# Key/value stage: context tiles of the third to last batch turned by VectorE and SBUF-to-SBUF transfers

## The reference

```python
k = (encoder_hidden_states @ Wk + bk).reshape(b, se, NKV, HD).transpose(0, 2, 1, 3)
v = (encoder_hidden_states @ Wv + bv).reshape(b, se, NKV, HD).transpose(0, 2, 1, 3)
...
k = _rmsnorm(k, kn_w)
```

## Time and profile before

| | us |
|---|---|
| median of 3 runs | 859.6 (857.96 to 860.68) |
| the profiled execution's own time | 860.1 |
| its span | 858.4 |
| PE busy | 796.0 (93%) |
| DVE busy | 574.9 (67%) |
| ACT busy | 473.4 (55%) |
| POOL busy | 538.6 (63%) |

### The profile page before, as it was taken

How to read it: one execution, slowest core, us unless ns; L and a number is a source line. 1 busy time by engine, 2 the same in 40 slices (tenths; PEclk the granted TensorE clock), 3 DMA queues, 4 the chain that set the end, 5 groups by cost and what they waited for, 6 DMA issues and landing times. The chain is left out here.

```text
span 858.4 us, 14128 instructions
## 1 busy us (share of the span) xinstructions
PE 796.0 (93%) x3968; PEld 655.0 (76%) x3968; DVE 574.9 (67%) x1049; ACT 473.4 (55%) x1620; POOL 538.6 (63%) x547
## 2 busy tenths in 40 slices
PE   5999987999999999999999999999977799878997
PEld 4888865887787788788788888787865677766786
DVE  4545456688688688688688688688677587664522
ACT  4554446656656656656656656656643265553440
POOL 2333355676776776776776776776856297554880
PEclk9999997999999999999999999999998799999999
DMA  6566563222322322332322332332345655312520
GB/s 220 198 211 203 184 211 99 62 86 61 98 86 61 98 86 60 98 86 60 98 87 59 98 89 58 98 88 59 93 135 171 209 191 189 118 34 90 199 96 25
DMA packets 85002, 97.66 MB, mean 114 GB/s; under 512 B 8113, under 2 KB 48177, under 8 KB 84977
## 3 DMA queue, kind: packets, MB, share of 16 engines
q1 hardware_dynamic: 84400, 95.52, 36.7%
q0 software_dynamic: 576, 1.84, 0.6%
HBM read 63.77 MB, written 17.30 MB: 94 GB/s over the span
## 5 line engine op out<-in xcount | busy, mean ns | idle before, releaser
L1049 ACT ACTIVATE p_row<-s_row,neg_max 128x128 f32<-128x128 f32 x256 | 100.0, 395 | 73.7 <-DVE neg_max L1332 73.7
L875 POOL TENSOR_TENSOR wp_lo<-raw,wp_hi 128x2048 fp32r<-128x2048 f32 (+1 forms) x24 | 104.1, 4344 | 49.7 <-ACT wp_hi L941 49.6
L799 POOL TENSOR_TENSOR p_row<-p_row,p_inv 128x512 f32<-128x512 f32 x64 | 66.8, 1044 | 107.1 <-DVE p_inv L1347 107.1
L1725 PE MATMUL b_y<-wo_hi,oT_hi 128*128 128x512 f32 x256 | 107.2, 419 | 6.2 <-DVE oT_lo L1236 5.6
L1727 PE MATMUL b_y<-wo_hi,oT_lo 128*128 128x512 f32 x256 | 101.3, 396 | 0.0
L1726 PE MATMUL b_y<-wo_lo,oT_hi 128*128 128x512 f32 x256 | 101.1, 395 | 0.0
L1725 PE MATMUL b_q<-wq_hi,xT_hi 128*128 128x512 f32 x248 | 97.6, 394 | 0.0
L1727 PE MATMUL b_q<-wq_hi,xT_lo 128*128 128x512 f32 x248 | 97.3, 392 | 0.0
L1726 PE MATMUL b_q<-wq_lo,xT_hi 128*128 128x512 f32 x248 | 97.2, 392 | 0.0
L941 ACT ACTIVATE oT_hi<-b_o 128x512 fp32r<-128x512 f32 x64 | 38.3, 599 | 100.6 <-PE b_o L1727 98.6
L831 POOL TENSOR_TENSOR pT_lo<-raw,pT_hi 128x512 fp32r<-128x512 f32 x62 | 80.8, 1304 | 0.3 <-ACT pT_hi L941 0.3
(11 more groups left out here) (304 smaller groups left out, 2215.4 us busy)
## 6 DMA issues: line engine op xcount, KB each, us to landing
raw<-raw SPq DMA_DIRECT2D x248, 64.0 KB, 2.1
cx<-in_ctx_dram SPq DMA_DIRECT2D x16, 256.0 KB, 2.7
raw<-in_L_xattn_Wq_dram SPq DMA_DIRECT2D x16, 256.0 KB, 2.8
raw<-in_L_xattn_Wo_dram SPq DMA_DIRECT2D x16, 256.0 KB, 3.3
v_store<-v_out SPq DMA_DIRECT2D x16, 256.0 KB, 3.4
k_store<-k_out SPq DMA_DIRECT2D x16, 256.0 KB, 2.0
xr<-in_x_dram SPq DMA_DIRECT2D x16, 256.0 KB, 3.2
k_raw<-k_store SPq DMA_DIRECT2D x16, 256.0 KB, 2.8
```

The costliest lines, as they stand in the source:

```text
L799: pool.tensor_tensor(p_row[:], p_row[:], per_head(p_inv, S), ALU.mult).then_inc(p_normed, 1)
L875: pool.tensor_tensor(wp_lo[n % NSLOT][:, part, :], raw[RAW_OF[n]][:, part, :], wp_hi[n % NSLOT][:, part, :].bitcast(fp32), ALU.subtract).t ...
L1049: e = act.activation(place, row, ACT.Exp, bias=neg_max[:, h:h + 1], accum_out=p_sum[:, h:h + 1])
L1725: pe.matmul(dst, left[0], right[0], start=start, stop=False)
```

## The change

Batches 0 and 1 are turned by PE as before. For the batches 2 to 15:

- DVE turns cx by a block transpose into c_tr, a quarter of raw[0] (`c_turn(b + 2)` at the start of DVE's batch b). It waits for cx to have landed and for the four transfers of the tile before to have landed. DVE's cT_lo is left out for these batches, also the one that stood behind the stage's loop (`turn_c(NB - 1, 1)`).
- SP then issues four transfers of 64 KB from c_tr into cT_in (two buffers, in raw[0] and raw[1]), `load_turned(b + 2)`. They stand ahead of the context load (now of batch b+4), of the weights and of the two stores. The contexts 2 and 3 are loaded ahead of the loop. The load of x for the attention stage stands one turn of the loop earlier.
- ACT makes cT_hi of batch b+1 from cT_in instead of b_xT (`high_c`), POOL makes cT_lo (`c_low`), ahead of the rest of its batch.
- PE's list has no turn of the context any more after batch 1.
- The semaphore pT_loaded is named turned_loaded and counts the context's transfers too, so the attention stage's waits on it are shifted by 64 x 14.

The diff, cut to its core (the renamed semaphore's other places are left out):

```diff
@@ -184,6 +184,8 @@
+        c_tr = raw[0][:, 2, :].rearrange("p (j c s) -> p j c s", j=4, c=DC)
+        cT_in = [tile_.rearrange("p (i c s) -> p i c s", i=4, c=DC) for tile_ in (raw[0][:, 3, :], raw[1][:, 2, :])]
@@ -572,18 +574,34 @@
             def load_x(b):
                 sp.dma_start(xr[:], x_rows[bass.ds(b * S, S), :]).then_inc(x_loaded, 16)
 
+            def load_context(b):
+                sp.wait_ge(c_turned, b - 1)
+                sp.dma_start(cx[b % 2][:], ctx_rows[b * S:(b + 1) * S, :]).then_inc(cx_loaded[b % 2], 16)
+
+            def load_turned(b):
+                sp.wait_ge(c_turned, b + 1)
+
+                if b >= 4:
+                    sp.wait_ge(c_lo, b - 1)
+                for i in range(4):
+                    sp.dma_start(cT_in[b % 2][:, i].rearrange("p c s -> p (c s)"),
+                                 c_tr[32 * i:32 * i + 32].rearrange("d j c s -> d j (c s)")
+                                 ).then_inc(turned_loaded, 16)
+
+            load_context(2)
+            load_context(3)
             for b in range(NB - 1):
-                if b < NB - 2:
-                    sp.wait_ge(c_turned, b + 1)
-                    sp.dma_start(cx[b % 2][:], ctx_rows[(b + 2) * S:(b + 3) * S, :]
-                                 ).then_inc(cx_loaded[b % 2], 16)
                 if b == 0:
                     load_weights(0)
-                load_weights(b + 1)
-                if b == NB - 3:
+                if b < NB - 2:
+                    load_turned(b + 2)
+                if b < NB - 4:
+                    load_context(b + 4)
+                if b == NB - 4:
 
                     sp.wait_ge(c_turned, NB - 1)
                     load_x(0)
+                load_weights(b + 1)
                 if b > 0:
                     store_v(b - 1)
                     store_k(b - 1)
@@ -762,14 +780,30 @@
 
+            def by_block(tile_):
+                return tile_[:].rearrange("p c (i s) -> p c i s", i=4)
+
+            def c_low(b, par):
+                pool.wait_ge(c_hi, b + 1)
+
+                pool.wait_ge(c_lo, b)
+                pool.tensor_tensor(by_block(cT_lo[par]), cT_in[par].rearrange("p i c s -> p c i s"),
+                                   by_block(cT_hi[par]).bitcast(fp32), ALU.subtract).then_inc(c_lo, 1)
+
             def kv_batch(b):
                 pool.wait_ge(k_squared, b + 1)
                 rsqrt(k_ss[:], k_rs[:], eps_head[:], k_summed, k_rooted, b + 1)
                 pool.wait_ge(k_rooted, b + 1)
                 pool.tensor_tensor(k_row[:], k_row[:], per_head(k_rs, HD), ALU.mult).then_inc(k_normed, 1)
 
-            with pool.Fori(0, NB - 2) as b:
-                kv_batch(b)
+            kv_batch(0)
+            with pool.Fori(0, NB // 2 - 2) as g:
+                for par in (0, 1):
+                    c_low(2 * g + 2 + par, par)
+                    kv_batch(2 * g + 1 + par)
+            c_low(NB - 2, 0)
+            kv_batch(NB - 3)
+            c_low(NB - 1, 1)
 
             def x_norm_stat(b):
 
@@ -947,6 +981,13 @@
+            def high_c(b, par):
+                act.wait_ge(turned_loaded, 64 * (b - 1))
+
+                act.wait_ge(v_projected, b - 1)
+                copy(cT_hi[par][:].rearrange("p c (i s) -> p c i s", i=4),
+                     cT_in[par].rearrange("p i c s -> p c i s")).then_inc(c_hi, 1)
+
@@ -970,8 +1011,10 @@
             def kv_batch(b, par, nth, first, last):
-                if not last:
-                    turn_c(b + 1, 1 - par)
+                if first:
+                    turn_c(1, 1)
+                elif not last:
+                    high_c(b + 1, 1 - par)
@@ -1022,7 +1065,7 @@
-                act.wait_ge(pT_loaded, 64 * (t + 1))
+                act.wait_ge(turned_loaded, 64 * (t + 1 + NB - 2))
                 wait(act, mixed, t)
@@ -1241,6 +1284,12 @@
+            def c_turn(b, par, nth):
+                dve.wait_ge(cx_loaded[par], 16 * nth)
+
+                wait(dve, turned_loaded, 64 * (b - 2))
+                dve.transpose(c_tr, cx[par][:].rearrange("p (c d j) -> p j c d", c=DC, j=4)).then_inc(c_turned, 1)
+
@@ -1271,17 +1320,21 @@
-            def kv_batch(b, par):
-                turn_c(b + 1, 1 - par)
+            def kv_batch(b, par, nth):
+                c_turn(b + 2, par, nth)
                 key_rows(b)
                 value_rows(b)
                 weights_low(b, par)
 
-            kv_batch(0, 0)
+            turn_c(1, 1)
+            dve.wait_ge(c_turned, 2)
+            dve.wait_ge(kv_w_hi, 2 * DC)
+            dve.wait_ge(kv_w_lo, 2 * DC)
+            kv_batch(0, 0, 2)
             with dve.Fori(0, NB // 2 - 2) as g:
-                kv_batch(2 * g + 1, 1)
-                kv_batch(2 * g + 2, 0)
-            kv_batch(NB - 3, 1)
+                kv_batch(2 * g + 1, 1, g + 2)
+                kv_batch(2 * g + 2, 0, g + 3)
+            kv_batch(NB - 3, 1, NB // 2)
 
 
             def x_statistics(b):
@@ -1334,7 +1387,7 @@
 
-                wait(dve, pT_loaded, 64 * t)
+                dve.wait_ge(turned_loaded, 64 * (t + NB - 2))
                 dve.transpose(p_tr, p_row[:].rearrange("p h (j d) -> p j h d", j=4)).then_inc(p_turned, 1)
@@ -1391,7 +1444,6 @@
 
-            turn_c(NB - 1, 1)
             key_rows(NB - 2)
@@ -1761,9 +1813,9 @@
 
-            def kv_batch(b, par, next_nth, first=False, between=None):
-                if between is None:
-                    turn_c(b + 1, 1 - par, next_nth)
+            def kv_batch(b, par, first=False, between=None):
+                if first:
+                    turn_c(1, 1, 1)
                 pe.wait_ge(c_lo, b + 1)
@@ -1775,10 +1827,10 @@
             turn_c(0, 0, 1)
-            kv_batch(0, 0, 1, first=True)
+            kv_batch(0, 0, first=True)
             with pe.Fori(0, NB // 2 - 1) as g:
-                kv_batch(2 * g + 1, 1, g + 2)
-                kv_batch(2 * g + 2, 0, g + 2)
+                kv_batch(2 * g + 1, 1)
+                kv_batch(2 * g + 2, 0)
             def project_q(t, b, quad, bank=b_q, banks=1):
@@ -1859,7 +1911,7 @@
             turn_x(0)
-            kv_batch(NB - 1, 1, None, between=first_query)
+            kv_batch(NB - 1, 1, between=first_query)
```

More of the change, by code:

```diff
@@ L372, in xattn_then_routed_ffn @@
         p_turned = sem("p_turned")
-        pT_loaded = sem("pT_loaded")
+        turned_loaded = sem("turned_loaded")
         pT_hi_done = sem("pT_hi_done")
@@ L627, in load_p @@
                                  p_tr[32 * i:32 * i + 32].rearrange("d j h s -> d j (h s)")
-                                 ).then_inc(pT_loaded, 16)
+                                 ).then_inc(turned_loaded, 16)
             def attend(b, first, last):
```

## The result

| | before | after |
|---|---|---|
| median, us | 859.4 (4 runs) | 926.6 (4 runs, 925.3 to 927.2) |
| the profiled execution's own time | 860.1 | 926.1 |
| its span | 858.4 | 924.4 |
| mean granted TensorE clock | 0.981 | 0.951 |

The ratio is 1.078, with a 95% interval of 1.0759 to 1.0802: 67.2 us slower, where 51 were forecast. 926.6 lies 0.6 us above the range, and the interval (some 924.6 to 928.3 us) spans the range's upper end; against the forecast itself the change costs 16 us more. The direction, the ring and its order are as forecast; the size is not.

A forecast was written before the change was run, and what follows sets the result against it. The prediction took the v_out/v_store ring, just beside PE, to end the key/value stage. First step +5.1, twelve steps +41.9, context issues +4.7, end -0.6: +51.1 on 860.1, so 911 us, range 899 to 926.

The forecast's parts named there:

- the ring: Key/value stage: v_out, weights' low parts, SP's issues, v_store's landing, next v_out; 6.63 us a turn before, ends the stage.
- PE loses 14 turns: PE, key/value stage: 14 x 0.44 = 6.2 us less work, counted as 0 because PE already waited for v_out.
- Rival B: SP takes the four added issues in its idle time, so no change: 860 us; chance 0.02.
- Rival A: PE bounds the key/value stage, the ring does not; batch falls to 5.96 us, total 853.4 us; chance 0.05.
- The ring's new step: Key/value stage, per batch: 6.63 + 0.64 + 2.55 + 0.47 + 0.3 = 10.6 us with a context load, 10.1 without.
- Landing, +0.3: v_store, issue to landing: 0.3 us longer per turn behind the added transfers, bounds -0.5 and +1.0.
- DVE, +0.64: Block transpose of batch b+2 on DVE lies in the ring: 704 ns less 0.06 us overlap, +0.64 us per turn.
- Context issue, +0.47: SP's context load issue, now in the ring: 0.43 us, +0.47 with its gap, in ten steps, +4.7 us together.
- the end, -0.6: End of the key/value stage: DVE has no cT_lo ahead of xn, for which PE waited 0.72 us; -0.6 us.
- The signs to look for: v_out rows 10 to 11 us apart, each behind v_store; PE waiting 4 to 5 us per batch; fourteenth v_out near 156.
- Rival C: PE's clock falls to 1.2 GHz in the new ring's gaps, matmuls slow down: about 920 us; chance 0.12.
- Rival D: Transfers pile up: v_store lands 1 us or more later, issues take 3.00 us; 17 us more, 928; chance 0.08.

The follow-up runs named there:

- v_store first: The changed kernel with v_store of batch b-1 issued at the head of SP's loop turn, ahead of transfers, context and weights: 863.2 us, ratio 1.0052.
- every ring open: The changed kernel with v_store issued first on SP, k_row ahead of DVE's block transpose, and two buffers each for v_out and k_out: 855.6 us, ratio 0.9959.
- the straight read: The changed kernel with DVE's block transpose reading runs of 32 neighbouring elements instead of every fourth: 921.4 us, ratio 1.0712.

## Why the prediction was wrong in size

**What held.** *PE loses 14 turns*, counted at 0: yes, the saving shows only where the rings are open. *cT_hi and cT_lo*, 0: yes, ACT waits 9.3 us for the turned transfers and nobody waits for that. *I see one ring*: yes, the order of its rows is the forecast's, and v_store first takes 63 us away. *Four issues*, 2.55: 2.53. The rival with PE as the bound is out for this kernel: the ring turn was 6.63 and became 11.5. Rival B's price, no change, was nearly right where it applies: the same four transfers in SP's idle time cost 2.3 us. Rival A's 853.4 for an open ring was near: with every ring open the change takes 855.6, which is 3.7 of the 6.2 us in the medians.

**What failed** is the step *The ring's new step: ... = 10.6 us*. The turn shown above took 11.54 us and the mean one 11.39. The sum of what was added, 3.96, lacked 0.95 us of the measured 4.91, by three terms in the main:

- *Landing, +0.3*, measured +0.86. "Nearer to no change because the engines were only 61% busy" took a mean over the batch for the moment of the store. The context load and the weights, 768 KB, are issued in the 1.7 us right ahead of it, and with the context moved away the landing falls from 4.3 to 3.5 us.
- *DVE, +0.64*, measured +0.83 in the ring, because the block transpose takes 1.09 us and not the 0.70 of "the same operation on p_row". It reads every fourth element, which the name of the operation in the row doesn't tell; the straight read takes 0.71. (0.2 us of the difference is given back, as DVE's two weight rows follow each other at once in after.)
- *Context issue, +0.47*, measured 0.64. I took the duration of the issue where it stood before, in SP's idle time; behind four other issues it takes 0.59.

The mean step over all twelve is (167.34 - 30.64)/12 = 11.39 us, with 10.43 for the last one, which has no context or x load; forecast were 10.5 in the mean. Twelve steps make 10.5 us of the miss and the first step 0.5 (v_out 1 at 30.64, not 30.1; the text's own terms for that step add to 5.0, not 5.1): the fourteenth v_out stands at 167.34, 62.7 us later than before, where the text had about 51.7. The other 3.3 of the 66.0 us between the spans come behind it. There *the end, -0.6*, does not show: PE gains nothing as xn is still made 3.7 us after that v_out (171.06). The second xn of the attention stage is 63.7 us later than before, so some 2.3 us arise after it, in small pieces; what they are was not tested. So "behind the stage: 0" was a little wrong too.

**The signs to look for** came in kind, each v_out behind a wait for v_store and PE waiting once per batch, but not in size. v_out rows stand 11.4 us apart (10 to 11 in the text), the fourteenth is at 167.34 (near 156), v_store was issued 5.3 us after the transpose's start (4.7), and PE waits 3.3 us per batch (4 to 5), since part of its work ran at the low clock.

**Rival C** named something that does happen and does not decide: the clock falls in every batch and is 0.81 over the stage, and PE waits 43.4 us for v_out all the same. Its own sentence, that a low clock costs nothing while the work fits into the ring's step, holds with 11.4 us even for work at 1.2 GHz. **Rival D** had half of one of its two parts: the store lands 0.56 later than taken, where D wanted 1 us or more, and the issues stay at 2.5 us. That its 928 is so near to 926.6 is luck: the rest came from terms that it didn't name, DVE, the context issue and what lies behind the stage. The page of the Trainium skill on transfers (DMA: Bandwidth & Descriptors, "Anatomy of one DMA — SWDGE (gpsimd) path") would have put v_store at an estimated 2.6 us; the trace's 4.3 is further from it than the 3.4 of before. Its 2.0 us and bytes over 436 GB/s are fitted to transfers that GpSimd issues, and v_store is issued by SP, so neither trace speaks for or against the page; nor does the fit have a term for the 768 KB issued just ahead.

**The range** was drawn in from a computed 895 to 928, as "not all terms go one way together". The three named above did: each was taken from rows of a less loaded place than the one it moved to, or of a simpler access.

## What to carry to other kernels

A buffer that is stored and then written again closes a ring through the queue that stores it. When work is put on that queue, follow the ring first: the same four issues cost 2.3 us outside it and 34 inside, and moving one store (or giving it a second buffer) was worth 63. After opening a ring, look for the same ring over two batches, and through the other store, before blaming bandwidth: only with all of them open did the change pay, 855.6 against 859.3. When an operation's or a landing's duration is taken from another place in the kernel, compare its access pattern and what is issued right ahead of it.

## What the runs showed of the hardware

- DVE's block transpose of 128x512 float32: 706 ns from elements that lie together, 1094 ns from every fourth.
- wq_lo and wo_lo on DVE, 0.68 us, take about 1.53 in the turns of the first opened kernel in which they run beside POOL's k_row, which itself takes 1.48 (65.22) to 1.58 there and 1.04 in after. That the two slow each other was not tested alone.
- SP takes 0.43 us to issue the context in its idle time and 0.59 behind the turned issues, and 0.62 for each of the four SBUF-to-SBUF transfers. In the kernel with all rings open SP's issues of one batch took 5.3 us (64.20 to 69.45), near PE's 5.96.
- k_store lands after 2.1 us in the median where it is issued 2.4 us behind v_store (before), and after 4.5 where it is issued 0.5 us behind it.
- PE's matmuls fell to the pace of the granted clock 0.50 (0.43 us each) in each of thirteen batches with gaps of 2.7 to 4.0 us, from 1.2 us behind the gap at the latest, and came back to 0.23 us within the batch.
